# Copies ahead of rows, weights behind a scatter and a turn without fills in an attention and mixture-of-experts kernel

## The reference

```python
x = x + xattn(layernorm(x), ctx, ctx, ...)   # softmax(q k^T) v Wo, residual, norm with gamma and beta
x = x + ffn(layernorm(x), ...)

def ffn(x):                                   # T = 4096 tokens, E = 32, TOP_K = 4
    scores = softmax(xf @ Wg)
    weights, indices = top_k(scores, TOP_K)
    for e in range(E):                        # tokens that chose e, up to a capacity
        out = swiglu(xf[tok], W1[e], W2[e], W3[e]) * w[:, None]
        y = y.at[tok].add(out)
    return y + swiglu(xf, Ws1, Ws2, Ws3)      # swiglu: silu(x @ w1) * (x @ w3) @ w2
```

## Time and profile before

| | us |
|---|---|
| three runs | 752.91, 755.36, 756.23 |
| their median | 755.36 |
| the profiled execution | 751.79 |
| its span, from the first to the last instruction | 750.0 |
| TensorE busy in the span | 725.6 |

### The profile page before, as it was taken

The page is one execution under the profiler, slowest core; times in us unless marked ns, Lnnn a source line. Parts: engine busy times, 40 slices in busy tenths (PEclk is TensorE's granted clock), DMA queues, the critical chain, the costliest instruction groups (busy, mean ns, idle before and its releaser), DMA issues.

```text
span 750.0 us, 18767 instructions
## 1 busy us (share of the span) xinstructions
PE 725.6 (97%) x4227; PEld 569.6 (76%) x4228; DVE 513.6 (68%) x1684; ACT 461.9 (62%) x1818; POOL 376.6 (50%) x373
## 2 busy tenths in 40 slices
PE   6998999999999999998999999999999999999997
PEld 5765777777777777776775578798999999999655
DVE  4865547385967868594879665565666666666798
ACT  2666777777786768776761426566666666666300
POOL 1002251325666666666467747765666666666300
PEclk9999999999999999999999999999999999999999
DMA  8720273323445454559937958987777777766998
GB/s 323 249 69 13 87 219 118 128 99 139 157 144 175 160 172 149 197 194 373 350 128 268 388 177 297 312 286 230 232 236 225 238 224 226 235 195 194 415 412 336
DMA packets 100847, 164.46 MB, mean 219 GB/s; under 512 B 11493, under 2 KB 82227, under 8 KB 99251
## 3 DMA queue, kind: packets, MB, share of 16 engines
q1 hardware_dynamic: 86911, 121.81, 49.1%
q0 software_dynamic: 13824, 41.96, 15.3%
q10 hardware_dynamic: 52, 0.01, 0.0%
HBM read 90.01 MB, written 78.97 MB: 225 GB/s over the span
## 4 chain that ended last, share of the span: by engine, by line
PE 80%; issue 4%; ACT 4%; DMA 4%; DVE 3%; POOL 3%; SPq 2%; DVEq 0%; ACTq 0%; POOLq 0%
PE psum L1901 16%; PE psum L1779 15%; PE psum L1673 15%; PE psum L1609 9%; PE psum L1908 8%; PE psum L1811 7%; PE psum L1827 3%; PE psum L1632 3%; ACT sm L975 2%; POOL expert_lists L810 2%; DMA xblk<-expert_lists 2%; PE psum L1647 1%; DVE big L1570 1%; PE psum L1640 1%; SPq L470 1%
## 5 line engine op out<-in xcount | busy, mean ns | idle before, releaser
L853 POOL DMA_INDIRECT y_d<-sm,yrow x160 | 154.1, 963 | 91.9 <-DVE yrow L1542 70.3
L1901 PE MATMUL psum<-xbT,w_now 128*128 128x128 f32 x1280 | 170.3, 276 | 1.2 <-issue 0.8
L975 ACT ACTIVATE sm<-psum,nmax 128x77 f32<-128x77 f32 x512 | 158.2, 371 | 4.7 <-DVE nmax L1189 4.6
L824 POOL TENSOR_TENSOR sm<-sm,sinv 128x1232 f32<-128x1232 f32 x32 | 71.9, 2248 | 176.2 <-DVE sinv L1196 176.2
L1901 PEld LDWEIGHTS psum<-xbT,w_now 128*128 128x128 f32 x1280 | 155.5, 192 | 3.9 <-issue 2.6
L810 POOL DMA_INDIRECT expert_lists<-rows,slot x128 | 125.5, 981 | 57.8 <-issue 35.9
L1779 PE MATMUL psum<-big,pT 128*128 (+1 forms) x640 | 143.5, 379 | 0.6 <-ACT pT L986 0.6
L1673 PE MATMUL psum<-big,xnT 128*128 (+2 forms) x384 | 139.3, 510 | 0.8 <-ACT sm L975 0.8
L1779 PEld LDWEIGHTS psum<-big,pT 128*128 128x128 f32 x640 | 119.1, 190 | 15.7 <-issue 0.8
L975 ACT ACTIVATION_READ_ACCUMULATOR sm<-psum,nmax 128x1 f32 x512 | 129.6, 253 | 0.0
L1673 PEld LDWEIGHTS psum<-big,xnT 128*128 128x128 f32 x384 | 69.9, 190 | 57.1 <-issue 51.5
(11 more groups left out here) (212 smaller groups left out, 945.0 us busy)
## 6 DMA issues: line engine op xcount, KB each, us to landing
xblk<-expert_lists SPq DMA_DIRECT2D x160, 160.0 KB
y_d<-zero SPq DMA_DIRECT2D x32, 512.0 KB, 3.8
big<-y_d SPq DMA_DIRECT2D x8, 2048.0 KB, 18.1
big<-in_L_ffn_W SPq DMA_DIRECT2D x16, 320.0 KB, 6.6
expert_lists<-expert_lists SPq DMA_DIRECT2D x32, 160.0 KB
xin<-in_x SPq DMA_DIRECT2D x36, 128.0 KB, 2.7
xres<-in_x SPq DMA_DIRECT2D x8, 512.0 KB, 5.5
x_d<-x SPq DMA_DIRECT2D x8, 512.0 KB, 2.7
```

The source lines that it names most:

```text
L824: pool.tensor_tensor(e3, e3, sinv[:, t % 2, :].unsqueeze(2).to_broadcast([P, NH, SK]), ALU.mult).then_inc(s["probs_ready"], 1)
L853: pool.indirect_dma_start(out=y_d, out_offset=bass.IndirectOffsetOnAxis(ap=yrow[:, q:q + 1], axis=0), in_=eo[:, q, :], in_offset=None).the ...
L975: last = nc.scalar.activation(sm[:, t % 2, h * SK:(h + 1) * SK], head_scores(h, h + 1), ACT.Exp, bias=nmax[:, t % 2, h:h + 1], accum_out=s ...
L1901: last = mm(bank(2 + q % 2)[:, i * P:(i + 1) * P], w_now[:, q % 2, i, k, :], xbT[:, q % 2, k, :], start=k == 0, stop=k == KC - 1)
```

## The change

It has three parts. ScalarE copies the turned probabilities before it writes the first two tiles' rows, in every group. SyncE also waits for the scatters of group 3 (`lists_ready[1]`) before the first lot of weights in group 7, the three loads that stood ahead of the lots go out after the first three tiles' transfers, and GpSimd issues five scatters at t = 1 and three at t = 2 instead of four and four. `AHEAD` is 6 instead of 5, and the sixth turn is fetched without fills.

```diff
-    AHEAD = 5
+    AHEAD = 6
...
-            load_xg(0)
-            load_xg(1)
-            load_x2g(2)
             sp.wait_ge(s["scores_psum"], (NT - 2 * TG) * SB)
             sp.wait_ge(s["out_psum"], NT - 2 * TG)
+
+            sp.wait_ge(lists_ready[1], 16 * TG * TOPK * (NG // 2 - 2))
             for t in range(TG):
                 load_experts(EARLY + (MIDDLE - EARLY) * t // TG, EARLY + (MIDDLE - EARLY) * (t + 1) // TG, "weights")
                 step(NG // 2 - 1, 1, t)
+                if t < 2:
+                    load_xg(t)
+                elif t == 2:
+                    load_x2g(2)
...
-            for i in range(2, AHEAD):
+            for i in range(2, AHEAD - 1):
                 load_turn(i, fill_lists(sp, fill_at_regs, (i - 1) * FILLS))
-            assert (AHEAD - 1) * FILLS == E and FILLS == NX and MID == 4
+            load_turn(AHEAD - 1)
+            assert (AHEAD - 2) * FILLS == E and FILLS == NX and MID == 4
             sp.wait_ge(s["filled"], 16 * E)
...
                 if t < 3 and live(jh, ph):
-                    scatter_rows(jh, ph, *((7 if live(j, p) else 5, 8), (8, 12), (12, 16))[t])
+                    scatter_rows(jh, ph, *((7 if live(j, p) else 5, 8), (8, 13), (13, 16))[t])
...
-                last_tile = isinstance(j, int) and num(j, p, t) == NT - 1
-                if t == 3 and live(*g1) and not last_tile:
-                    make_rows(*g1, (0, 1))
                 if live(jm, pm):
                     move_pT(jm, pm, tm)
-                if last_tile:
+                if t == 3 and live(*g1):
                     make_rows(*g1, (0, 1))
```

## The result

The changed kernel takes **748.14 us** (median of 6 runs, 747.01 to 748.58), the kernel before beside it 754.65 us (6 runs, 752.91 to 757.92). The ratio is 0.9918 (95% interval 0.9899 to 0.9936): 6.2 us or 0.8% faster, by more than the 0.5% that can be told. Predicted were 752.1 us, a range from 749.2 to 755.4, and no difference that can be told as the likeliest case.

What follows compares the result with a forecast made beforehand. TensorE, busy 725.6 of 750.0 us, was taken as the bound, so only its waits could be won. Terms of -2.27 and -1.03 us, -3.3 together, took the median 755.36 to 752.1 us, range 749.2 to 755.4.

Steps and rivals of the forecast that it cites:

- Term A: End of group 6 in the attention stage: TensorE's two waits, for rows and normalized input, both go, -2.27 us.
- The 0.43 us: Late tile at the end of group 6: the rest of 2.27 us beside both waits, TensorE's restart, gaps not wholly counted.
- Nothing was lost behind the new wait: SyncE's group 7 queue, delayed 6.8 us by waiting for the scatter, was counted at nothing; 20 us of DMA room.
- third rival: Last tile: weights ending 6.8 us later delay group 4's last scatter, TensorE waits for its rows; 756.9 us, chance 0.08.
- GpSimd's extra scatter: Thirteenth scatter moved to the second tile: takes 1.27 us of 1.72 us of waiting there, 0.45 us left.
- Term B: Sixth turn of blocks: its first block no longer waits once fetched without fills, -1.03 us, bounds 0 and -1.03.
- rival of longer waits: Scatter or fills land one to three microseconds later in ordinary runs, so 4.3 to 6.3 us go, say 750.0; chance 0.22.

Runs made afterwards that it cites:

- pool_only: The kernel before with only GpSimd's scatters changed, five in the second tile and three in the third instead of four and four: 752.35 us, ratio 0.9971.
- stores_late: The changed kernel with the last two stores of base rows moved from the first two turns of blocks into the sixth: 748.29 us.
- late_scatter: The kernel before with three scatters in the second tile and five in the third instead of four and four: 755.52 us, ratio 1.0023.
- same_third: The kernel before, unchanged, for a third trace: 753.18 us in one run.
- order_weights: The changed kernel without its sixth turn, so ScalarE's order and the weights behind the scatter: 749.97 us, ratio 0.9951 to the kernel before.
- better: The changed kernel with six list fills in each of four turns instead of eight in three, and two base-row stores later: 748.83 us.

## Why the prediction was wrong

By 18 runs (748.14, 747.69 and 747.96) the changed kernel's median is 747.84 us, 6.0 below the 753.87 of before; the three ratios allow 3.8 to 8.7. What failed is the sum, not the mechanism of its two terms. It started 1.5 us too high, its terms A and B came from one trace in which both waits were short, and fell short by 0.2 and 0.5, and what TensorE's clock loses behind a wait, 0.9 us here, was a term that it did not have. Step by step:

**The start of the sum was 1.5 us too high.** The three runs shown had a median of 755.36; 69 later ones 753.87. From there the sum gives 750.6, and the true gain is 2.7 us more than it.

**Term A: right in mechanism, 0.2 us too small.** The tile went to 10.21 us; both waits went, and the weights started late, as worked out. In three traces of before the tile took 12.48, 12.77 and 12.82, so the term is 2.5 instead of 2.27. Two steps in it were wrong without harm. The 0.43 us beside the two waits was put down to gaps that aren't wholly counted as waits. The two gaps are just the 0.77 and 1.07 us (342.72 to 343.49 and 344.15 to 345.22), so the 0.43 us must lie in what surrounds them: in the rows of after the rows, the input and the value sum each start 0.16 us before the matmuls ahead of them end, which a wait takes away twice, and the rows and the input took 0.06 us longer each in before. And a scatter started 1.27 us sooner was to land at 341.1 even with the weights in flight; pool_only shows it landing no sooner. Of the two halves of the Trainium skill's rule (DMA: Bandwidth & Descriptors, Queues, rings and completion order) this agrees with the second, that a completion mark comes after all earlier writes of its engine. That taking turns alone would have let the earlier start count is argued; no run here looks at the marks themselves.

**Nothing was lost behind the new wait: right.** The rows of the last tile were to wait some 1.3 us (381.0 to 382.3) in the third rival's working, hidden from TensorE. They waited 1.28 us, and TensorE's 0.75 us are those of before. The scatter began at 377.15 and let go at 383.02, after 5.87 us, somewhat more than the worst that the working assumed; the last tile had room for that. GpSimd's extra scatter fitted too, with 0.20 us left where 0.45 were expected.

**Term B: right in mechanism, too small by 0.5 us.** The block is regular now. But 2.58 us was the shortest of eight such blocks: in the seven traces without a fall at that place they took 2.58 to 3.62, 3.03 in the mean, so the term is 1.5 instead of 1.03. The runs themselves give 0.8 for it alone and 1.8 on top of the other parts.

**What no term held: the clock.** Falls cost before 1.0 us in the mean of its runs (754.03 over all 69, 753.03 over the 39 without), and the changed kernel 0.1, so 0.9 went with the change. The mean clocks of the two kinds of runs, 0.9964 and 0.9989, account for 1.9 of the 2.3 us between them; the rest may be longer waits that go with the falls. I had read the granted clock as full nearly throughout and didn't ask what TensorE's waits do to it in other executions. The rival of longer waits was the nearest, in time (750.0) and in cause; it had no price for what follows a wait. From a start of 753.87 its 4.3 to 6.3 us would have given 749.6 to 747.6, with the measured time inside.

**What else moved.** The first tile of group 6 took 12.55, 12.24 and 12.55 us in before, 12.12 to 12.14 in three traces of after: 0.3 us. It is VectorE's late start behind a return of its loop, in which the trace shows no cause (before, then after):

```profile
304.49 1.50 DVE L1189 TENSOR_REDUCE nmax<-psum 128x12 f32<-128x924 f32 x2 [4.13 <-issue]
```

```profile
305.02 1.50 DVE L1190 TENSOR_REDUCE nmax<-psum 128x12 f32<-128x924 f32 x2 [3.69 <-issue]
```

The runs name no part of the change as its cause: order, weights and scatters alone each show 12.06 to 12.10, the sixth turn alone 12.61, stores_late 12.34 and late_scatter 11.47.

**The account:** 2.5 + 1.5 + 0.9 + 0.3 = 5.2 of 6.0 us. The 0.8 us left are less than half the width of any of the three intervals, 1.4 us or more, and stay open. The same items also cover why the parts alone win more than their tiles show. For the order the tile gives 1.2, the first tile of group 6 0.4 and the rarer falls (1 of 12 for 12 of 29, at 2.3 us) 0.8, 2.3 together of 2.7. For the weights it is 2.5, 0.35 and 0.95, 3.8 where 3.4 were measured. Both differences are within the intervals.

**The profiled pair agreed by chance.** Its tiles and blocks gave 2.27, 0.43 (first tile of group 6) and 1.55 us (all blocks), 4.25 together, and the changed kernel's preparation happened to be 0.95 us longer (its first value sum starts at 76.93 instead of 75.98; in two other executions of it at 74.97 and 76.26). The prediction said that the terms would be right and the runs lose elsewhere if the span fell by 3.3 us and the runs did not; they fell by more, and part of what they had lost was at these very waits.

## What to carry to other kernels

One profiled execution is one draw, and where it is faster than all runs shown its waits for transfers may be short ones, as they were here: size such a term from several traces, and set the sum on the median of many runs. A wait of TensorE can cost more than its length: here the clock fell behind some of them, for 1.7 us more. Where a small transfer lands late behind bulk loads, starting it a little earlier may do nothing, as here with 1.27 us; hold the loads back until it has landed, if their consumers are far off.

## What the hardware showed

The granted clock fell to 1.2 GHz right behind waits of TensorE (two of 1.06 and 1.07 us in a row, and single ones of 1.89 to 2.52 us), for 1.7 us lost each time. In other traces two waits of 1.10 and 1.07 us in a row (same_third) and single ones of 1.75 (order_weights) and 1.86 us (better) brought no fall. The landing of an indirect scatter followed the start of the weights (10.6 to 11.0 us behind it in six traces), not its own start, which lay 5.0 us behind them in five and 3.7 in one; started 6.2 us behind them, it landed at 12.45. VectorE stood still for 3.2 to 4.2 us at one return of its loop with nothing in the trace to wait for.
